# End of a gated linear attention: head norm ahead of the last mask, output product right behind its transposes

## The reference, cut to what matters

```python
# first attention, 4 heads, keys 32 wide, values 64 wide
S = jnp.exp(gt)[:, None] * S + kt[:, None] * vt[None, :]      # one state for each head, step by step
o_t = qt @ S
o = o * rsqrt(mean(o * o, axis=-1) + EPS) * rms_w             # norm for each head
x = x + (o.reshape(b, t, DV) * silu(x @ Wg)) @ Wo
# cross-attention, 16 heads of width 8, the values are of the context
x = x + softmax(q k^T / sqrt(8)) v @ out_w.T + out_b          # q, k, v from layernorm(x), ctx, ctx
```

## Time and profile before

| | |
|---|---|
| median of 3 runs | 471.76 us (470.08 to 473.48) |
| the profiled execution, its own time | 471.7 us |
| its span, first to last instruction | 469.8 us |
| mean granted clock of TensorE over the span | 0.985 |
| busy over the span: PE, DVE, ACT, POOL | 92%, 76%, 62%, 46% |

### The profile page before, as it was taken

How to read it: one execution, slowest core, us unless ns; L and a number is a source line. 1 busy time by engine, 2 the same in 40 slices (tenths; PEclk the granted TensorE clock), 3 DMA queues, 4 the chain that set the end, 5 groups by cost and what they waited for, 6 DMA issues and landing times.

```text
span 469.8 us, 13121 instructions
## 1 busy us (share of the span) xinstructions
PE 433.6 (92%) x4542; PEld 308.8 (66%) x4542; DVE 359.3 (76%) x976; ACT 289.6 (62%) x688; POOL 213.8 (46%) x552
## 2 busy tenths in 40 slices
PE   7999887997789998699999999999999997998887
PEld 6554565766657777366666676667676765887747
DVE  3797659785779989887777878777777867567785
ACT  3753426884388874677677777777777766413450
POOL 5160011660223557056766767567666676440200
PEclk9999899998999999999999999999999999999998
DMA  7399935500001131000000000000000000000001
GB/s 219 74 98 100 98 42 183 179 4 0 1 3 35 45 91 35 1 1 18 5 18 2 0 17 17 0 0 0 0 0 0 2 1 2 1 3 1 1 0 46
DMA packets 15621, 15.80 MB, mean 34 GB/s; under 512 B 1348, under 2 KB 12859, under 8 KB 15579
## 3 DMA queue, kind: packets, MB, share of 16 engines
q1 hardware_dynamic: 15579, 15.24, 16.0%
HBM read 10.52 MB, written 4.72 MB: 32 GB/s over the span
## 4 chain that ended last, share of the span: by engine, by line
PE 73%; DVE 17%; ACT 5%; issue 3%; DMA 1%; POOL 0%; SPq 0%; DVEq 0%; ACTq 0%; POOLq 0%
PE bank L972 16%; PE bank L1490 12%; PE bank L1442 10%; PE bank L1365 5%; PE bank L1286 3%; PE bank L1273 3%; PE bank L1483 3%; PE bank L1361 3%; PE bank L1173 2%; PE bank L1380 2%; PE bank L1624 2%; DVE Y L1654 1%; PE bank L1075 1%; PE bank L1089 1%; PE bank L977 1%
## 5 line engine op out<-in xcount | busy, mean ns | idle before, releaser
L882 ACT ACTIVATE SN<-SN,nmx 128x512 f32<-128x512 f32 x128 | 92.7, 725 | 9.8 <-DVE nmx L2027 7.5
L972 PE MATMUL bank<-cs,SN 128*128 128x128 f32 x512 | 67.3, 274 | 3.3 <-DVE Z L2020 1.6
L972 PEld LDWEIGHTS bank<-cs,SN 128*128 128x128 f32 x512 | 57.2, 141 | 18.1 <-issue 12.1
L1442 PE MATMUL bank<-TK,TQ 64*128 64x512 f16 x384 | 52.6, 380 | 1.4 <-DVE TK L1990 1.4
L553 POOL TENSOR_TENSOR CTW<-YT 128x128 f32<-128x128 f32 x64 | 29.6, 463 | 51.1 <-DVE YT L2025 50.5
L2012 DVE CUSTOM_DVE_ANT_0 SN<-bank,strip 128x512 f32<-128x512 f32 x64 | 43.3, 677 | 1.2 <-PE bank L1442 0.6
L2027 DVE CUSTOM_DVE_ANT_0 SN<-bank,strip 128x512 f32<-128x512 f32 x64 | 43.6, 681 | 0.0
L2020 DVE COPY PTO<-bank 128x512 f32<-128x512 f32 x32 | 22.2, 692 | 20.9 <-PE bank L1490 19.2
L893 ACT COPY PTO<-bank 128x512 f32<-128x512 f32 x32 | 18.8, 586 | 26.0 <-PE bank L1490 26.0
L977 PE MATMUL bank<-ones 128*128 128x128 f32 x228 | 33.6, 304 | 1.0 <-POOL konst L401 1.0
L2020 DVE COPY Z<-bank 128x512 f32<-128x512 f32 x32 | 22.1, 692 | 15.9 <-PE bank L1490 14.0
(11 more groups left out here) (328 smaller groups left out, 976.5 us busy)
## 6 DMA issues: line engine op xcount, KB each, us to landing
bias_rows<-biasr SPq DMA_DIRECT2D x1, 4096.0 KB, 45.2
band<-bias_rows SPq DMA_DIRECT2D x1, 3072.0 KB, 11.4
wqkv<-in_twqkv SPq DMA_DIRECT2D x8, 192.0 KB, 2.7
w1s<-in_w SPq DMA_DIRECT2D x8, 128.0 KB, 2.1
w2s<-in_w SPq DMA_DIRECT2D x8, 128.0 KB, 2.2
wB<-in_wb SPq DMA_DIRECT2D x1, 753.0 KB, 6.0
wA<-in_wa SPq DMA_DIRECT2D x1, 520.0 KB, 4.8
X<-in_x SPq DMA_DIRECT2D x2, 256.0 KB, 3.3
```

What stands on the lines that cost most here:

```text
L882: sc.activation(p, p, ACT.Exp, bias=nmx[:, r % RING, h:h + 1], scale=-1.0, accum_out=psm[:, r % RING, h:h + 1]).then_inc(sm["exp_ready"], 1)
L972: return nc.tensor.transpose(out_, in_, ident[0:n, 0:n])
L1442: ins = mm(bank[2 * (s % 2) + h][:, :], TQ[u][r, q_part, S * b + P * qt:S * b + P * qt + P], TK[u][r, k_part, S * b:S * b + S], start=(k = ...
```

## The change

It reorders the end of the GLA on PE and DVE, and halves one filler:
- DVE: `head_norm(0)` goes from behind `gate_out(5)` to in front of `gla_mask(7)`; `value_blocks()` goes from in front of the norm's `norm_rows(1, 0, ...)` to behind `head_norm(1)`.
- PE: `gla_o` is split into `gla_inside` (masked scores) and `gla_before` (state). For the last tile the order is now transposes of half 0, inside product, output product of half 0, state product, spreading of the values; it was transposes, spreading, output product, inside product, state product. For the other tiles the order is the same.
- PE: `keep_busy(3, 8)` behind it becomes `keep_busy(3, 4)`.

ACT, POOL and SP are unchanged. The kernel after has four more lines from here on in PE's part, and so other line numbers.

```diff
@@ -1064,22 +1064,24 @@
                     mm(bank[2 + r][:, 0:DV], KPT[CH * r:CH * r + CH, i, :], V[CH * r:CH * r + CH, i, :],
                        start=True, stop=True).then_inc(sm["kv_mm"], 1)
 
-            def gla_o(i):
+            def gla_inside(i):
+
                 pe.wait_ge(sm["kpt_ready"], min(i, 1) + 1)
                 pe.wait_ge(sm["am_ready"], i + 1)
                 if i >= 2:
                     pe.wait_ge(sm["ob_ready"], i - 1)
-                o = bank[4 + i % 2]
-                firsts = 2 * i % CB == 0
                 for h in range(GH):
-                    ins = mm(o[:, GV * h:GV * h + GV], AM[:, i % 2, h, :], V[:, i, GV * h:GV * h + GV],
-                             start=(h == 0), stop=False, skip_group_check=True)
+                    mm(bank[4 + i % 2][:, GV * h:GV * h + GV], AM[:, i % 2, h, :], V[:, i, GV * h:GV * h + GV],
+                       start=(h == 0), stop=False, skip_group_check=True)
+
+            def gla_before(i):
+
                 for r in range(2):
                     c = 2 * i + r
                     if c % CB == 0:
                         continue
                     pe.wait_ge(sm["st_ready"], c // CB * (CB - 1) + c % CB)
-                    ins = mm(o[CH * r:CH * r + CH, 0:DV], QP[:, CH * c:CH * c + CH], ST[:, c % 4, :],
+                    ins = mm(bank[4 + i % 2][CH * r:CH * r + CH, 0:DV], QP[:, CH * c:CH * c + CH], ST[:, c % 4, :],
                              start=False, stop=True, skip_group_check=True)
                 ins.then_inc(sm["o_mm"], 1)
 
@@ -1117,19 +1119,21 @@
 
             gla_a(0)
             keep_busy(5, 2)
-            for i in range(NT):
+            for i in range(NT - 1):
                 gla_kv(i)
-                if i + 1 < NT:
-                    gla_a(i + 1)
-                if i == NT - 1:
-                    gla_t(0)
-                    spread_values()
-                    gla_out(0)
-                gla_o(i)
+                gla_a(i + 1)
+                gla_inside(i)
+                gla_before(i)
                 if i == 0:
                     keys_t(1)
                 if i + 2 < NT:
                     gla_vg(i + 2)
+            gla_kv(NT - 1)
+            gla_t(0)
+            gla_inside(NT - 1)
+            gla_out(0)
+            gla_before(NT - 1)
+            spread_values()
 
             def queries(g):
 
@@ -1174,7 +1178,7 @@
                              PT[0:n, i % 2, c, P * j:P * j + P], start=(c == 0), stop=(c == 2))
                 return ins
 
-            keep_busy(3, 8)
+            keep_busy(3, 4)
             norm_half(1, Y, 0)
             queries(0)
             gla_t(1)
@@ -1788,20 +1792,20 @@
             keys_out(1)
             for i in range(NT):
                 gla_state(i)
+                if i == NT - 2:
+                    head_norm(0)
                 if i + 1 < NT:
                     gla_mask(i + 1)
                 if i >= 1:
                     gate_out(i - 1)
                 if 1 <= i < TG:
                     weight_scales(i - 1)
-                if i == NT - 2:
-                    head_norm(0)
             gla_residual(0)
             norm_stats(1, 0, X)
-            value_blocks()
             norm_rows(1, 0, X, Y)
             gate_out(NT - 1)
             head_norm(1)
+            value_blocks()
 
             def ctx_norm(i):
                 dve.wait_ge(sm["rc_ready"], i + 1)
```

## The result

| | before | after |
|---|---|---|
| median, 16 executions each | 471.17 us (468.01 to 473.97) | 469.60 us (468.03 to 470.13) |
| ratio | | 0.9958, 95% interval 0.9938 to 0.9978 |
| profiled execution | 471.7 us | 468.24 us |
| its span | 469.8 us | 466.3 us |
| mean granted clock over the span | 0.985 | 0.993 |

The change makes the kernel faster by 0.4% (2.0 us by the ratio), a small gain but clear of the noise. The two profiled executions differ by 3.5 us, and the sum of 3.63 us was worked out for such a pair; the forecast of the median was 468.4, and the measured median is 1.2 us above it. That the medians differ by less than the traces is the main thing the experiments had to explain.

What follows compares the result with a forecast made beforehand. The prediction saw a chain through DVE, PE and ACT at the GLA's end, with PE at half clock. 4.02 + 0.26 − 0.65 = 3.63 us off 471.7 gave 468.1, put at 468.4; own range 467.2 to 469.3, whole 466.5 to 471.3.

Steps and rivals of the forecast that it cites:

- the sum of 3.63 us: Total predicted gain against the profiled execution: 4.02 at the residual, plus 0.26 at the norm, minus 0.65 for VB.
- The head norm: End of the GLA: head norm ahead of the last mask lets PE's transposes start at 53.70, 1.23 us earlier.
- Residual at 58.09, 4.02 earlier: End of the GLA: DVE starts the residual after the output product at 58.09 instead of 62.11.
- The rival in which it falls all the same: Clock falls behind the shorter 0.43 us gap; residual at 59.4, gain 2.3, 469.4 us; chance 0.12.
- Order 1.4, clock 2.6: Split of the 4.02 us at the residual: 1.4 from the order, 2.6 from PE at full clock.
- step 2: PE's inside product between transposes and output product, spreading behind: residual 4.02 us earlier, 1.4 of it order.
- step 4: Norm after the residual, VB moved out and ACT's squares done earlier: Y 4.28 us earlier, 0.26 beyond the residual's gain.
- Norm and Y: Norm after the residual without VB in it: Y starts at about 60.73 against 65.01, 4.28 us earlier.
- VB behind the head norm costs 0.65: VB multiplies behind the second head norm delay `query_low` to 65.76 instead of 65.11; 0.65 us lost, kept to the end.
- The slower rival: Four fewer keep-busy matmuls let the clock fall from 61.2 us on; 471.5, or 473.1 if it lasts; chance 0.05.
- the rival that its fall is not in most executions: Most executions of before lack the clock's fall at the GLA's end; only order gains, 1.0 us, 470.7; chance 0.2.
- The third rival: Later half-clock stretch, 112.27 to 115.68, shrinks or goes: up to 1.7 us more gain, 466.4; chance 0.13.

Runs made afterwards that it cites:

- filled gap: Six keep-busy matmuls added in PE's gap in front of the first transposes, against the kernel before: 469.04 us median, ratio 0.9962.

## Why the prediction was right

- *The head norm.* Predicted: PE starts at 53.70 instead of 54.93. Measured: 53.68. The mask and gate cost the inside product 0.22 us of waiting, not 0.1, and nothing behind it.
- *Residual at 58.09, 4.02 earlier.* Measured: 58.09. The clock stayed at 1.00, as the rows with gaps of 0.6 to 0.7 us had suggested. The rival in which it falls all the same did not come: none of the ten traces of kernels with the head norm early has a fall between 53 and 62 us.
- *Order 1.4, clock 2.6.* The filled gap gives 59.31, so 1.2 and 2.8. The spreading at full clock takes 1.42 us where I had taken 1.6.
- *PE's new order.* The 1.4 of step 2 is 1.23 of the head norm and so 0.2 of PE's order; the runs leave it nothing at the residual. The 0.2 us of step 4, through ACT's squares, it has. What I missed is that at full clock the old order fits under ACT's copies as well as the new one, and so that the head norm's move is enough by itself.
- *Norm and Y.* Predicted 60.73, measured 60.70. Transposes of Y at 61.87 (61.9), not held up by the filler, which ended at 61.00.
- *VB behind the head norm costs 0.65.* `query_low` at 65.77 (65.76), and putting VB into the idle time brought it to 65.07 and the span from 466.3 to 465.6. From `query_low` to the end it is 400.5 us after and 400.4 before, so nothing behind absorbed or added to it.
- *The slower rival.* With four fillers less, the clock stays at 1.00 from 61 to 72 us in all four traces of after. The one near variant with a fall at 72.74 has the eight fillers.
- *The sum.* 3.63 us predicted against the profiled execution, 3.46 measured. The terms hold one by one, but that the whole came so close is in part luck with the pair: against the second trace of before, the same trace of after has 1.3 us less span, not 3.5.

Where it was loose is the step from one execution to the median. The forecast of 468.4 had a range of its own of 467.2 to 469.3, and the measured 469.60 lies above it, inside the whole range of 466.5 to 471.3; the gain is 0.4% and not 0.7%. I took the profiled execution of before for a typical one and gave 0.2 to the rival that its fall is not in most executions, with 1.0 us for the order alone; the filled gap puts that at 0.8. But neither case describes the median. Both traces of before have the fall, with 1.3 us between them (how many of its executions do, two traces can't tell), and 17 of 30 executions of after have a mean clock under 0.992, that is, more half clock than the 6.8 us of its fastest ones. So the gain in the medians is between 1.6 and 3.3 us depending on the set, and the ratio on which the result rests is 0.9958. The third rival, in which the stretch of 112.27 shrinks or goes, did not come in the profiled pair (109.47 to 112.88, as long as before and behind the same wait). It had a true part all the same: before's second trace has no half-clock stretch at 112, but another at 133.7. That is scatter, though, and not an effect of the change.

## What to carry to other kernels

Before moving work off a stretch that looks bound by TensorE, look at the granted clock in it. If it is low, find the wait in front of the fall and shorten or fill it; here that was 2.8 of the 3.6 us by which `query_low` came earlier in the first two traces, and the reordered matmuls were worth 0.2. Where an engine idles for a known time in front of an operation, put the displaced work ahead of that operation and not behind it. Compare medians only with the mean clock of each execution beside them, and take differences in time from traces in which the clock is low in the same places: the same mean clock is not enough.

## What the hardware showed that I had not expected

- The place and length of a half-clock stretch differ between executions of the same kernel: behind the same wait of 1.66 us it was 54.2 to 61.1 and 55.2 to 58.6 in two traces of before; behind the same wait of 2.51 us it was 3.4 us and 10.2 us long in two traces of after. The Trainium skill, "TensorE: Matmul & The Clock Gate", section "What's actually happening", says that the place at which the clock changes varies from run to run of one kernel, of matmuls at a kernel's start. Here the traces show it in the middle of a kernel, and executions of one kernel with different mean clocks lie over 2.3 us (30 of after) and over 7 us (73 of before).
- PE had been idle for under 1 us (53.27 to 54.24) when the clock fell in the first trace, behind a tile of the GLA without its values and gate product. In two other traces it fell only when PE was at work again, 0.35 us (before) and 1.03 us (head norm put back) behind the same gap. Twelve passes of filler in that gap kept the clock in the one trace that has them. Seven waits of 0.22 to 0.89 us between 53 and 71 us passed at 1.00 in the four traces of after.
- In the spreading of the values a pass over 256 columns starts every 0.43 us where the clock is low (2.56 us for six, 56.69 to 59.25) and every 0.24 where it is high (1.42 us for six, 54.62 to 56.04 with the head norm alone).
